# Third layer's edges: nine products in one instruction, a cross product ahead of the first map, features scaled in advance, relu logits

## What is computed

```python
def _cg_tp(s, v, y0, y1, w_ss, w_sv, w_vs, w_vv0, w_vv1):
    out_s = jnp.concatenate([w_ss * s * y0[:, None], w_vv0 * (jnp.einsum('eci,ei->ec', v, y1) / SQRT3)], axis=-1)
    out_v = jnp.concatenate([(w_sv * s)[:, :, None] * y1[:, None, :], w_vs[..., None] * v * y0[:, None, None],
                             w_vv1[..., None] * (jnp.cross(v, y1[:, None, :]) / SQRT2)], axis=1)
    return out_s, out_v

w1 = rbf @ W_rbf                                   # rbf: 16 radial features of each edge
m1_s, m1_v = _cg_tp(msg_s, msg_v, y0, y1, *split(w1))
a = (m1_s @ W_alpha).reshape(e, H, AS_)
a = jnp.where(a > 0, a, 0.2 * a)
a = jnp.sum(a * alpha_dot, axis=-1, keepdims=True) # the logits, softmaxed over the edges of a node
val_s = m1_s @ Ws_val
val_v = jnp.einsum('ecx,cd->edx', m1_v, Wv_val)
val_v = val_v * jax.nn.sigmoid(val_s @ Wg)[..., None]
m2_s, m2_v = _cg_tp(jax.nn.sigmoid(val_s), val_v, y0, y1, ...)   # a second product and a second map follow
```

## Time and profile before

| | before |
|---|---|
| median of 3 runs | 12669.28 us (12666.13 to 12681.18) |
| the profiled execution, its own time | 12702.04 us |
| its span, first to last instruction | 12700.3 us |
| mean granted TensorE clock | 0.791 |
| busy: PE, PEld, DVE, ACT, POOL | 73%, 57%, 69%, 36%, 64% of the span |
| `edge_tables` | 75 to 166 us of the span |
| `layer2_edges` | 7290 to 9830 us of the span |

### The profile page before, as it was taken

How to read it: one execution, slowest core, us unless ns; L and a number is a source line. 1 busy time by engine, 2 the same in 40 slices (tenths; PEclk the granted TensorE clock), 3 DMA queues, 4 the chain that set the end, 5 groups by cost and what they waited for, 6 DMA issues and landing times. The chain is left out here.

```text
span 12700.3 us, 220425 instructions
## 1 busy us (share of the span) xinstructions
PE 9229.7 (73%) x44798; PEld 7244.6 (57%) x44798; DVE 8713.2 (69%) x21701; ACT 4529.6 (36%) x11637; POOL 8172.7 (64%) x8692
## 2 busy tenths in 40 slices
PE   2899999973655666666664578888887465999985
PEld 2888888863545322222223477777776454565654
DVE  4677777777643555555554389999999764667763
ACT  1455555540012222222221267777776001333331
POOL 4788888864843788888882176666664582666650
PEclk7777777776865777777776589999898786899995
DMA  3455555434620688888885233333332562333331
GB/s 91 106 114 115 113 113 114 115 85 112 170 74 15 111 131 131 131 130 131 130 132 141 102 79 81 81 81 81 81 81 67 129 170 59 84 87 87 93 87 41
DMA packets 1339110, 1293.91 MB, mean 102 GB/s; under 512 B 504078, under 2 KB 1142018, under 8 KB 1338374
## 3 DMA queue, kind: packets, MB, share of 16 engines
q0 software_dynamic: 347904, 594.12, 25.6%
q1 hardware_dynamic: 913580, 653.03, 20.0%
q10 hardware_dynamic: 77530, 45.68, 1.2%
HBM read 781.38 MB, written 510.73 MB: 102 GB/s over the span
## 5 line engine op out<-in xcount | busy, mean ns | idle before, releaser
L664 POOL DMA_INDIRECT e_gs<-tab_src,e_ix x1568 | 1708.1, 1089 | 763.2 <-issue 429.9
L664 POOL DMA_INDIRECT e_gd<-tab_dst,e_ix x1568 | 1610.7, 1027 | 477.8 <-issue 474.4
L715 PE MATMUL e_psS<-e_rows,e_same 128*128 128x480 f32 x1568 | 1113.6, 876 | 848.2 <-DVE e_same L689 848.2
L603 PE MATMUL e_psF<-w_ident,e_F 128*128 128x128 f32 x6272 | 1293.0, 315 | 246.9 <-ACT e_F L1822 233.0
L733 POOL DMA_INDIRECT acc<-e_sums,e_row x784 | 1247.5, 1591 | 239.0 <-issue 206.7
L715 PEld LDWEIGHTS e_psS<-e_rows,e_same 128*128 128x128 f32 x1568 | 430.6, 293 | 1541.7 <-issue 1514.7
L1642 POOL DMA_INDIRECT e_g<-tab_src,e_er x976 | 970.1, 994 | 525.1 <-issue 284.1
L633 ACT ACTIVATE e_FT<-e_psF 128x384 f32<-128x384 f32 (+1 forms) x2352 | 1078.0, 458 | 538.5 <-PE e_psF L603 526.4
L1431 PE MATMUL s_psS<-s_wv,s_hot 128*128 128x168 f32 (+1 forms) x3904 | 800.0, 361 | 615.2 <-POOL s_wv L1389 242.6
L603 PEld LDWEIGHTS e_psF<-w_ident,e_F 128*128 128x128 f32 x6272 | 895.5, 170 | 389.9 <-issue 346.0
L1431 PEld LDWEIGHTS s_psS<-s_wv,s_hot 128*128 128x128 f32 x3904 | 694.3, 228 | 720.4 <-issue 529.5
(11 more groups left out here) (471 smaller groups left out, 23529.8 us busy)
## 6 DMA issues: line engine op xcount, KB each, us to landing
s_val<-val SPq DMA_DIRECT2D x488, 320.0 KB
val<-e_O SPq DMA_DIRECT2D x392, 320.0 KB, 2.7
acc<-w_zeros SPq DMA_DIRECT2D x392, 139.5 KB
n_ag<-acc SPq DMA_DIRECT2D x56, 960.0 KB
e_krow<-in_src_t SPq DMA_DIRECT2D x196, 256.0 KB
sums<-e_total SPq DMA_DIRECT2D x244, 192.0 KB
e_es<-in_es SPq DMA_DIRECT2D x196, 130.0 KB
e_gs<-tab_src,e_ix POOLq DMA_INDIRECT x1568
```

The source lines that it names most:

```text
L603: last = nc.tensor.transpose(psF[:, P * g:P * g + P], F[:, k, P * g:P * g + P], ident[:, :])
L664: pool.indirect_dma_start(into[t][u][:, k, :], None, tables[t], bass.IndirectOffsetOnAxis(ix[u][:, t, k:k + 1], 0))\
L715: nc.tensor.matmul(psS[(k) % len(psS)], T["same"][u][:, k, :], values[:, k, :], start=True, stop=True)\
```

## The change

It is made of six edits.

1. `dve_message_products` takes the place of `dve_products` in this layer. One instruction forms all nine products of a message's three components with the three of `y1` (`nine`). The dot product is a reduction over three of them, the cross product two subtractions of the others, written behind the message (`crossed`, `msg` becomes 256 wide). The scalars' two products are one instruction.
2. `crossed_weights` and `pe_message_maps` lay out the first map anew: three matmuls of 164, 128 and 96 columns instead of 192, 96 and 96, the last two adding into one region. The result is 292 wide instead of 384. Behind the map only `tmp0 = u * y1` and one sum are left on DVE (L2058 and L2064 of the changed kernel).
3. The factor `y0` is taken out of the message. The radial weights of the two parts that carry it come from 16 further features, `es16 * y0`, so `es` has 32 rows and `l2_rbf` is 32 x 224. ACT's four instructions a step on `msg0` are gone.
4. `es16 * y0` is made once, in `edge_tables`: PE turns `y0`, ACT copies it out, SP stores it to DRAM (`y0_t`), and then in eight rounds SP loads a part of `es16` and of `y0` (eight DMAs each, every one of 16 partitions by 1,568 numbers), POOL multiplies 128 x 1568, and SP stores the product in eight DMAs. These stand on SP ahead of the store of `edge_rows`. A round may start when the stores of the round two before have landed.
5. The leaky relu is written as 0.2 a + 0.8 relu(a). The linear part becomes four further columns of the first map (160 to 163), filled in `setup`; the other is one instruction with `alpha_dot` already in it. The logits are one reduction and a sum of 16 numbers a partition.
6. `setup` has three more weight loads and five more small instructions on DVE.

The diff, cut to its core:

```diff
-    whole("l2_rbf", [16, 224], D["L2_gnn_W_rbf"])
+    tile("l2_rbf", [32, 224], *[((slice(r, r + 16), slice(a, b)), D["L2_gnn_W_rbf"][:, a:b])
+                                for r, a, b in ((16, 0, 64), (0, 64, 128), (16, 128, 160), (0, 160, 224))])
...
-    message_weights(tile, "l2", [(D["L2_gnn_W_alpha"], 0), (D["L2_gnn_Ws_val"], 64)], D["L2_gnn_Wv_val"], C1)
+    crossed_weights(tile, "l2", [96, 164], [((slice(0, 96), slice(0, 64)), D["L2_gnn_W_alpha"]), ((slice(0, 96), slice(64, 128)), D["L2_gnn_Ws_val"])],
+                    D["L2_gnn_Wv_val"])
...
-            scale("l2_t2", A, A, float(np.sqrt(0.5)))
+            scale("l2_t1", slice(96, 128), A, float(np.sqrt(0.5)))
+            scale("l2_t2", slice(0, 64), A, float(np.sqrt(0.5)))
+            link(nc.vector.tensor_tensor(slope[:, :], W["l2_t0"][0:96, 0:64], W["l2_adot"][0:96, :], ALU.mult))
+            link(nc.vector.tensor_reduce(W["l2_t0"][0:96, 160:164], slope[:, :].rearrange("p (h a) -> p h a", a=16), AX.X, ALU.add))
+            scale("l2_t0", A, slice(160, 164), 0.2)
+            scale("l2_adot", A, A, 0.8)
...
+        Q, CH = ET // 7, EPAD // 8
+        PART = CH // 8
+        psY, y0T = S.ps("psY", [Q, 2, 512]), S.sb("y0T", [Q, 7, P])
+        es2, y2 = ([S.sb(f"{name}{u}", [P, PART]) for u in range(2)] for name in ("es2", "y2"))
...
+        def scaled_out(sp, n):
+            u = n % 2
+            sp.wait_ge(sem("scaled"), n + 1)
+            for c in range(8):
+                at = bass.ds(CH * c + PART * n, PART)
+                sp.dma_start(D["es16_y0"][:, at], es2[u][16 * c:16 * c + 16, :]).then_inc(sem(f"scaled_out{u}"), 16)
...
+            y0_row = D["y0_t"].rearrange("t p -> (t p)")
+            for n in range(8):
+                u = n % 2
+                if n > 1:
+                    sp.wait_ge(sem(f"scaled_out{u}"), 128 * (n // 2))
+                for c in range(8):
+                    at = bass.ds(CH * c + PART * n, PART)
+                    sp.dma_start(es2[u][16 * c:16 * c + 16, :], D["es16"][:, at]).then_inc(sem(f"scaled_in{u}"), 16)
+                if n == 0:
+                    sp.wait_ge(sem("y0_T"), 2)
+                    sp.dma_start(D["y0_t"].rearrange("(g q) p -> q g p", q=Q), y0T[:, :, :]).then_inc(sem("y0_out"), 16)
+                    sp.wait_ge(sem("y0_out"), 16)
+                for c in range(8):
+                    at = bass.ds(CH * c + PART * n, PART)
+                    sp.dma_start(y2[u][16 * c:16 * c + 16, :], y0_row[at].partition_broadcast(16)).then_inc(sem(f"scaled_in{u}"), 16)
+                if n:
+                    scaled_out(sp, n - 1)
+            scaled_out(sp, 7)
...
             sp.dma_start(D["edge_rows"], row[:, :, :]).then_inc(sem("stored"), 16)
...
+                pool.wait_ge(sem(f"scaled_in{u}"), 256 * (n // 2 + 1))
+                nc.gpsimd.tensor_tensor(es2[u][:, :], es2[u][:, :], y2[u][:, :], ALU.mult).then_inc(sem("scaled"), 1)
...
+                act.wait_ge(sem("y0_turned"), n + 1)
+                a, b = 4 * n, min(4 * n + 4, 7)
+                nc.scalar.activation(y0T[:, a:b, :], psY[:, n, 0:P * (b - a)].rearrange("q (g p) -> q g p", p=P), ACT.Copy).then_inc(sem("y0_T"), 1)
...
+                last = nc.tensor.transpose(psY[:, g // 4, P * (g % 4):P * (g % 4) + P], attr[:, Q * g:Q * g + Q, 0], W["ident"][:, :])
...
+def crossed_weights(tile, tag, shape, scalar, vector):
+    wb, wc, wx = vector[0:64, :], vector[64:96, :], vector[96:128, :]
+    at = lambda r, c: (slice(r, r + C1), slice(c, c + C1))
+    tile(tag + "_t0", shape, *scalar)
+    tile(tag + "_t1", [128, 128], (at(0, 0), wc), (at(32, 32), wc), (at(64, 64), wc), (at(96, 0), wx))
+    tile(tag + "_t2", [128, 96], (at(0, 0), wx), (at(32, 32), wx), ((slice(64, 128), slice(64, 96)), wb))
...
+def dve_message_products(nc, dve, i, psW, msg, nine, dot, F, Y, S, free):
+    tt = nc.vector.tensor_tensor
+    v, crossed = msg[:, :, C0:CX], msg[:, :, CX:MSG_W]
+    dve.wait_ge(S.sem("msg"), i + 1)
+    tt(comp(nine[:, :, 0:3 * C1V]), bcast(v, 2, 3), bcast(Y, 3, C1V), ALU.mult).then_inc(S.sem("nine"), 1)
+    dve.wait_ge(S.sem("nine"), i + 1)
+    nc.vector.tensor_reduce(dot[:, :, :], nine[:, :, :].rearrange("p t (d c) -> p t c d", d=3)[:, :, 0:C1, :], AX.X, ALU.add)\
+        .then_inc(S.sem("dot"), 1)
+    tt(crossed[:, :, 0:C1], nine[:, :, 224:256], nine[:, :, 160:192], ALU.subtract)
+    tt(comp(crossed[:, :, C1:C1V], 2), comp(nine[:, :, 64:128], 2), comp(nine[:, :, 32:352], 2)[:, :, ::-1, 0:C1], ALU.subtract)\
+        .then_inc(S.sem("crossed"), 1)
+    dve.wait_ge(S.sem("weights"), i + 1)
+    wait(dve, *free)
+    tt(spread(F[:, :, X_A:], (X_W, TM), (X_B - X_A, 2), (1, C0)), comp(psW[:, :, 0:2 * C0], 2), bcast(msg[:, :, 0:C0], 2, 2), ALU.mult)
+    dve.wait_ge(S.sem("crossed"), i + 1)
+    tt(comp(F[:, :, X_C:X_C + C1V]), bcast(psW[:, :, 128:160], 2, 3), comp(v), ALU.mult)
+    tt(comp(F[:, :, X_X:X_X + C1V]), bcast(psW[:, :, 192:224], 2, 3), comp(crossed), ALU.mult)
+    dve.wait_ge(S.sem("dot"), i + 1)
+    tt(F[:, :, X_D:X_D + C1], psW[:, :, 160:192], dot[:, :, :], ALU.mult).then_inc(S.sem("products"), 1)
...
+def pe_message_maps(nc, pe, i, k, FT, o, W, w, rows, S, tag, ahead):
+    scalars = W[w + "_t0"].shape[1]
+    f = FT[:, k, :]
+    wait_apart(pe, S.sem(tag + "_FT"), i * TM + k + 1, S.sem("pe_passed"))
+    wait_apart(pe, S.sem(tag + "_O"), i * TM + k + 1 - ahead, S.sem("pe_passed"))
+    nc.tensor.matmul(o[:, 0:scalars], f[0:rows, 0:P], W[w + "_t0"][:, :], start=True, stop=True, skip_group_check=True)
+    nc.tensor.matmul(o[:, scalars:scalars + P], f[:, P:2 * P], W[w + "_t1"][:, :], start=True, stop=False, skip_group_check=True)
+    nc.tensor.matmul(o[:, scalars + C1:scalars + P], f[:, 2 * P:3 * P], W[w + "_t2"][:, :], start=False, stop=True,
+                     skip_group_check=True).then_inc(S.sem(tag + "_linear"), 1)
...
-                    sp.dma_start(es[u][:, :], D["es16"][:, bass.ds(i * ME, ME)]).then_inc(sem(f"es{u}"), 16)
+                    sp.dma_start(es[u][0:16, :], D["es16"][:, bass.ds(i * ME, ME)]).then_inc(sem(f"es{u}"), 16)
+                    sp.dma_start(es[u][16:32, :], D["es16_y0"][:, bass.ds(i * ME, ME)]).then_inc(sem(f"es{u}"), 16)
...
-                    act.wait_ge(sem("msg"), i + 1)
-                    wait(act, sem("products"), i)
-                    for k in range(TM):
-                        last = times_y0(msg0, msg, i, k)
-                    last.then_inc(sem("msg_y0"), 1)
...
-                    wait(dve, sem("dot"), i)
-                    wait(dve, sem("products2"), i - SECOND_IN + PRODUCT)
                     wait(dve, sem("products"), i)
-                    dve_products(nc, dve, i, psW, msg, msg0, prod, dot, F[u], Y(i)(0, 3), S,
-                                 (sem("msg"), i + 1), (sem("lin_turned"), (i - 1) * TM), (sem("msg_y0"), i + 1))
+                    dve_message_products(nc, dve, i, psW, msg, nine, dot, F[u], Y3(i), S, (sem("lin_turned"), (i - 1) * TM))
...
-                    nc.vector.scalar_tensor_tensor(out=lk[:, :, :], in0=a, scalar=0.2, in1=a, op0=ALU.mult, op1=ALU.max)\
-                        .then_inc(sem("leaky"), 1)
+                    nc.vector.scalar_tensor_tensor(out=lk[:, :, :], in0=a, scalar=0.0, in1=bcast(W["l2_adot"][:, :], 1, TM), op0=ALU.max,
+                                                   op1=ALU.mult).then_inc(sem("leaky"), 1)
...
-                    dve_cross(nc, dve, i, O[u], tmp, Y(i), 160, rotated(O[u], 288), 256, S, "cross")
-                    dve.wait_ge(sem("leaky"), 2 * i + 1)
-                    tt(lk[:, :, :], lk[:, :, :], bcast(W["l2_adot"][:, :], 1, TM), ALU.mult).then_inc(sem("leaky"), 1)
+                    C = comp(O[u][:, :, VEC:VEC + C1V])
+                    tt(comp(tmp[:, 0, :, :]), bcast(O[u][:, :, VEC + C1V:O_W], 2, 3), Y(i)(0, 3), ALU.mult).then_inc(sem("cross_first"), 1)
+                    dve.wait_ge(sem("leaky"), i + 1)
+                    wait(dve, sem("logit"), i)
+                    nc.vector.tensor_reduce(lsum[:, :, :], lk[:, :, :].rearrange("p t (h a) -> p t h a", a=16), AX.X, ALU.add)\
+                        .then_inc(sem("summed"), 1)
+                    dve.wait_ge(sem("cross_first"), i + 1)
+                    tt(C, C, comp(tmp[:, 0, :, :]), ALU.add).then_inc(sem("cross_done"), 1)
...
-                    dve.wait_ge(sem("leaky"), 2 * i + 2)
-                    dve.sem_inc(sem("dve_passed"), 1)
-                    nc.vector.tensor_reduce(logits[:, bass.ds(i * TM, TM), :], lk[:, :, :].rearrange("p t (h a) -> p t h a", a=16),
-                                            AX.X, ALU.add).then_inc(sem("logit"), 1)
+                    dve.wait_ge(sem("summed"), i + 1)
+                    tt(logits[:, bass.ds(i * TM, TM), :], lsum[:, :, :], O[u][:, :, LIN:VEC], ALU.add).then_inc(sem("logit"), 1)
```

More of the change, by code:

```diff
@@ L415, in _ @@
             sp.wait_ge(sem("stored"), 32)
+            for u in range(2):
+                sp.wait_ge(sem(f"scaled_out{u}"), 128 * 4)
         @block.gpsimd
```

(2 more changed lines are left out.)

45 lines of the change are left out of this document (27 added, 18 removed).

## The result

The changed kernel takes 12545.4 us (median of 4 runs, 12509.9 to 12564.5); the kernel before takes 12667.7 in the runs beside them. The ratio is 0.990 (95% interval 0.988 to 0.992): 122 us less, where the prediction had 75 less. Its profiled execution has a span of 12507.8 us. That is the lowest of the four runs, while the one profiled before lay 33 above its median, so I compare by stages.

What follows compares the result with a forecast made beforehand. DVE, 98% busy in the middle of `layer2_edges`, was taken as the bound. Terms: -237 (stage) + 160 (rounds in `edge_tables`) + 2 (setup) = -75, from a median of 12669.3 to 12594 us; range 12490 to 12680.

Steps and rivals of the forecast that it cites:

- DVE stays bound, step 11.45: In `layer2_edges`, DVE still sets the pace after the change, at 11.45 us a step and 98% busy.
- the 1.21 forecast: DVE's saving a step in `layer2_edges`: 1.29 us more for message products, 2.50 less behind the map.
- 237 us less in the stage: In `layer2_edges`, 1.21 us saved a step, times 196 steps, if DVE stays the bound.
- DVE is never idle there: In `layer2_edges`, the reason given for counting all of DVE's saved 1.21 us a step as on the path.
- times 196: In `layer2_edges`, the 1.21 us saved is counted for all 196 steps, giving 237 us.
- POOL needs 11.2, which fits, barely: In `layer2_edges`, POOL without its wait for DVE needs 11.2 us a step, under DVE's 11.45.
- the sign named for this: What would show the forecast wrong: DVE showing idle time on the gathers in `layer2_edges`.
- gathers held by DVE: Rival in `layer2_edges`: the wide product holds gathers, POOL needs 12.0 us a step; +33 us, 12702; chance 0.08.
- The rounds cost 160 us: In `edge_tables`, the new DMA rounds at 106 GB/s end at 326 us, passing DVE's 166.2 by 160.
- The lower case: In `edge_tables`, issuing binds the rounds (0.43 us a DMA, 83 us); end at 234 us, cost 68.
- PE and ACT bind: Rival in `layer2_edges`: the PE and ACT round stays 11.8 us, saving 169 us; total -7, 12662; chance 0.12.
- the quick rounds: Rival in `edge_tables`: DMAs to different partitions overlap, rounds cost 68 us; total -167, 12502; chance 0.20.

Runs made afterwards that it cites:

- d_half_gathers: The changed kernel with four gathers a step in `layer2_edges` instead of eight (rows of `tab_dst` left out); 12481.3 us, 64 less than the changed kernel.
- c_act_y0: The changed kernel with the edge scalar y0 again applied by ACT and no rounds in `edge_tables`; 12453.0 us, ratio to the kernel before 0.982.
- n: The changed kernel with the relu logits undone (leaky relu by DVE again); 12577.1 us, ratio to the kernel before 0.993.
- k: The changed kernel itself, unedited, run again in a later series; 12525.3 us, ratio to the kernel before 0.989.
- f_wide_rounds: The changed kernel with each round in three DMAs of 128 partitions instead of 24 of 16; 13938.7 us on the slower chip, 0.980 of the kernel before.

## Why the prediction was right, and where not

- *DVE stays bound, step 11.45*: right in the middle of the stage (11.46 to 11.50), and each size held: 1.35 for the nine, 0.60 from start to start for the 512-wide product, 0.09 for the 16-wide sum. DVE's own need fell a little more than the 1.21 forecast, from 12.64 to 11.33, and its waits for gathers took that back, so a part of the match is luck.
- *237 us less in the stage*: 210. The steps that failed are "DVE is never idle there" and "times 196". At the start gathers set the pace in both kernels (DVE waits 41.0 us in the first nine steps before, 37.7 in the first six after), so the saving, 1.15 a step from 7400 to 9500 (12.64 to 11.50), counts from there on, some 186 times. Draining the last steps after the last join gives about 10 back.
- *POOL needs 11.2, which fits, barely*: wrong in kind. POOL's need is not a constant; the wide product raised it to 11.46, level with DVE, and the sign named for this, DVE idle on gathers, is there (20.5 us in 1,800). The rival "gathers held by DVE" had the mechanism, and expected too much of it: all 0.8 us added, where the eight gathers grew by 0.3 a step. `d_half_gathers` prices what it costs, 0.17 a step. The forecast set the rival low because the means of the two tables' gathers differ by 0.12 us only. The comparison to make was with an undisturbed gather of 0.95: in the trace of the kernel before, from 7700 to 9415, 403 of 1,084 gathers took over 1.05, and all end 0.82 behind a DVE instruction. Those that start in L572 or L582 of `dve_cross` were 132 us longer there than 0.94 each; after, the largest share, 87 us, falls to the nine products.
- *The rounds cost 160 us*: 88. This is the term that was mis-sized, by taking the rate of 16 partitions from the `es8` loads. The lower case had the bound right (issue and landing), and was 20 short: the store of `y0_t` held the next loads for 14.3 us (112.33 to 126.59), not 6.5, and a round waits 3.4 for its stores, not 2.7. POOL's product took 3.48 us, not 4.2, hidden but for the last.
- *PE and ACT bind*: false on the usual chips, by `c_act_y0`; on the other chip the waits look like it.
- *The sum*: -210 - 10 + 90 = -130, measured -122. The forecast of -75 had both terms too large, the gain by 17 to 27 and the rounds by 72, and lay 47 too high for it; the quick rounds' -167 lay as far off on the other side. That -75 came within 47 us is luck in part: the two errors have opposite signs, and the one of the rounds, 72, is nearly as large as the forecast change itself.

By parts, then: the relu logits bring 41 us of the stage (n against k), and the cross product ahead of the map with the nine in one the rest, some 170 by subtraction; no run parts these two. The scaled features cost 60 to 108 by the medians, 89 by the traces, and bring nothing: the stage is as long without them, within 5 us.

## What to carry to other kernels

Where one engine's instructions hold up another's, the idle time of the one is no reserve for the other's growth: here wider DVE instructions with two inputs in SBUF made the gathers beside them longer. To see it ahead, compare the mean of such an instruction with its shortest. Price a new stream of DMAs by issue and landing as well as by its rate, and ask first whether an idle engine can do the same work under cover. When a saving is multiplied by a loop's count, take off the steps in which the pipeline fills.

## What was not expected of the hardware

- DMAs of 16 partitions, eight in a row and each to another group, moved 169 GB/s, the `es8` loads (8 partitions each, from two queues) 106, and whole-width ones in `f_wide_rounds` 237.
- All 431 gathers that took over 1.05 us end 0.82 us after a DVE instruction with two inputs in SBUF; one that starts in a row of these is held to the row's end in some places and not in others.
- The attention sums differ by 16 us, in opposite directions, with what was moved thousands of us earlier.
- One chip took 14205 us for what others do in 12670, and turned the order of two variants around (0.954 and 1.004 there, 0.993 and 0.983 elsewhere).
